# Contexts of a sequence taken in one visit instead of two, with eight buffers of turned probabilities

## The reference

```
x = emb[inp]                                   # token rows are gathered
q, k, v = x @ Wq.T + bq, x @ Wk.T + bk, x @ Wv.T + bv
scores = einsum('bhqd,bhkd->bhqk', q, k) / sqrt(16)      # 16 heads of 16
h = (softmax(scores) @ v) @ Wo.T + bo
n = layernorm(h);  Bu = (n @ B_w.T) @ C_w.T
h = h + sigmoid(n @ gate_w.T + gate_b) * exclusive_scan(decay, Bu)
h = h + layernorm(h) @ sign(weight).T
```

## Time and profile before

| | before |
|---|---|
| median of three runs | 829.03 us |
| the profiled execution's own time | 831.48 us |
| its span, first to last instruction | 829.4 us |
| mean granted TensorE clock | 0.979 |
| TensorE busy | 732.2 us (88%) |
| VectorE busy | 585.2 us (71%) |
| ScalarE busy | 580.9 us (70%) |
| GpSimd busy | 130.0 us (16%) |
| chain that ended last | PE 65%, issue 14%, DVE 9%, ACT 4% |

### The profile page before, as it was taken

The page is one execution under the profiler, slowest core; times in us unless marked ns, Lnnn a source line. Parts: engine busy times, 40 slices in busy tenths (PEclk is TensorE's granted clock), DMA queues, the critical chain, the costliest instruction groups (busy, mean ns, idle before and its releaser), DMA issues.

```text
span 829.4 us, 21108 instructions
## 1 busy us (share of the span) xinstructions
PE 732.2 (88%) x7047; PEld 650.2 (78%) x7047; DVE 585.2 (71%) x1307; ACT 580.9 (70%) x1643; POOL 130.0 (16%) x205
## 2 busy tenths in 40 slices
PE   1489999999999999999999999999999999999864
PEld 0378888888888888888888888888888888888754
DVE  4345677776677777777777787777777777787763
ACT  2178887777778877777787777777777777777710
POOL 7110111111110111111101111111011111100000
PEclk9889999999999999999999999999999999999977
DMA  4222223222322332223222312332232123322000
GB/s 128 89 90 77 90 91 103 69 73 91 102 91 91 97 101 61 72 95 101 93 93 92 101 56 71 101 101 89 88 101 95 56 76 101 101 89 81 23 13 26
DMA packets 56015, 69.67 MB, mean 84 GB/s; under 512 B 6768, under 2 KB 41648, under 8 KB 55984
## 3 DMA queue, kind: packets, MB, share of 16 engines
q1 hardware_dynamic: 52048, 60.48, 21.3%
q0 software_dynamic: 3072, 8.39, 4.9%
q10 hardware_dynamic: 864, 0.40, 0.2%
HBM read 10.52 MB, written 8.39 MB: 23 GB/s over the span
## 4 chain that ended last, share of the span: by engine, by line
PE 65%; issue 14%; DVE 9%; ACT 4%; SPq 3%; DMA 3%; POOL 1%; ACTq 0%; DVEq 0%; POOLq 0%
PE ps_g L623 32%; PE ps_t L695 10%; PE ps_g L672 8%; PE ps_c L623 7%; PE ps_s L623 6%; SPq L234 3%; DVE xn L519 2%; DVE h L583 2%; DVE gated L578 2%; ACT xTh L364 2%; PE ps_g L721 2%; DMA q_stack<-q_low 2%; SPq L239 1%; DMA gb_row<-in_gate_b 1%; DVE raw L452 1%
## 5 line engine op out<-in xcount | busy, mean ns | idle before, releaser
L338 ACT ACTIVATE probs<-ps_s,neg_max 128x128 f32<-128x128 f32 x1024 | 299.6, 400 | 73.6 <-DVE neg_max L486 73.6
L486 DVE TENSOR_REDUCE neg_max<-ps_s 128x4 f32<-128x512 f32 x256 | 176.4, 689 | 130.8 <-PE ps_s L623 128.7
L347 ACT COPY probsT<-ps_t 128x512 f32<-128x512 f32 x256 | 155.6, 608 | 43.1 <-PE ps_t L695 42.3
L695 PE MATMUL ps_t<-ident,probs 128*128 128x128 f32 x1024 | 154.4, 273 | 4.3 <-ACT probsT L347 4.2
L623 PE MATMUL ps_s<-k_stack,q_stack 128*128 128x256 f32 x512 | 124.3, 325 | 7.5 <-DMA q_stack<-q_low 7.5
L695 PEld LDWEIGHTS ps_t<-ident,probs 128*128 128x128 f32 x1024 | 119.6, 142 | 6.3 <-ACT probs L338 3.4
L286 POOL TENSOR_TENSOR rs<-ve,neg_half 128x2 f32<-128x2 f32 x32 | 22.2, 693 | 445.3 <-DVE ve L513 445.3
L623 PEld LDWEIGHTS ps_s<-k_stack,q_stack 128*128 128x128 f32 x512 | 78.1, 193 | 9.1 <-DMA q_stack<-q_low 9.0
L623 PE MATMUL ps_c<-probsT,v_aug 128*32 128x128 f32 x2048 | 83.1, 280 | 0.3 <-ACT probsT L347 0.3
L364 ACT CAST xTh<-ps_g 128x512 fp32r<-128x512 f32 x32 | 18.8, 586 | 77.8 <-PE ps_g L672 77.7
L721 PE MATMUL ps_g<-ident,ctx_raw 128*128 128x128 f32 x256 | 40.5, 281 | 34.5 <-ACT ctx_raw L357 34.5
(11 more groups left out here) (120 smaller groups left out, 1847.1 us busy)
## 6 DMA issues: line engine op xcount, KB each, us to landing
k_stack<-k_high SPq DMA_DIRECT2D x128, 128.0 KB, 2.4
q_stack<-q_high SPq DMA_DIRECT2D x64, 256.0 KB, 2.5
k_stack<-k_low SPq DMA_DIRECT2D x64, 128.0 KB, 2.3
q_stack<-q_low SPq DMA_DIRECT2D x32, 256.0 KB, 2.5
out<-y SPq DMA_DIRECT2D x32, 256.0 KB, 2.1
x_emb<-in_emb,id_col POOLq DMA_INDIRECT x64, 3.6
raw<-in_wkT SPq DMA_DIRECT2D x1, 256.0 KB, 3.0
raw<-in_wqT SPq DMA_DIRECT2D x1, 256.0 KB, 3.8
```

The costliest lines, as they stand in the source:

```text
L338: last = nc.scalar.activation(probs[s % 2][:, j], ps_s[s % 2][:, j * SEQ:j * SEQ + SEQ], ACT.Exp, bias=neg_max[s % 2][:, j:j + 1])
L347: nc.scalar.copy(probsT[st % 4][:], ps_t[:]).then_inc(act_pT, 1)
L486: nc.vector.tensor_reduce(neg_max[s % 2][:], ps_s[s % 2][:].rearrange("p (h k) -> p h k", h=HPS), axis=AX.X, op=ALU.max, negate=True).then ...
L695: last = nc.tensor.transpose(ps_t[:, j * SEQ:j * SEQ + SEQ], probs[st % 2][:, j], ident[:])
```

## The change

The two contexts per visit in four visits become four contexts per visit in two visits, in steps 2 and 6. The contexts of the second sequence (steps 4 to 7) run in step 2 of the next turn, those of the first (steps 0 to 3) in step 6. `probsT` gets a buffer for each of the eight steps, and a copy into it waits for the context of the same step one turn before. Nothing else moves; ScalarE's copies of `ps_c` keep their places.

```diff
-        probsT = [sb(f"probsT{p}", [P, HPS, SEQ]) for p in range(4)]
+        probsT = [sb(f"probsT{p}", [P, HPS, SEQ]) for p in range(8)]
@@ move_probsT
                         await_event(act, pe_pT, STEPS, pair, st + 1)
-                        await_event(act, pe_pv, STEPS, *after_four(pair, st))
-                        nc.scalar.copy(probsT[st % 4][:], ps_t[:]).then_inc(act_pT, 1)
-
-                def after_four(pair, st):
-                    p4, s4 = before(pair, st, 4)
-                    return p4, s4 + 1
+                        await_event(act, pe_pv, STEPS, pair - 1, st + 1)
+                        nc.scalar.copy(probsT[st][:], ps_t[:]).then_inc(act_pT, 1)
@@ context
-                    for back in (4, 3):
+                    for back in (6, 5, 4, 3):
@@
-                                      v_aug[vp][:, b, g * HPS + j], probsT[st % 4][:, j])
+                                      v_aug[vp][:, b, g * HPS + j], probsT[st][:, j])
@@ attention
-                    if s % 2 == 0:
+                    if s in (2, 6):
                         context(s)
```

## The result

| | before | after |
|---|---|---|
| median of 4 runs each | 828.74 us | 842.97 us |
| ratio to before, 95% interval | | 1.0169 (1.0152 to 1.0186) |
| the profiled execution's own time / its span | 831.48 / 829.4 us | 841.08 / 839.0 us |

The change makes the kernel 14 us slower. I had forecast 828.0 with a range of 810 to 836. The two profiled executions lie 9.6 us apart, less than the medians: the one of before took longer than any of its four timed runs, the one of after was the fastest of its four.

The account below looks back on a forecast made before the run. TensorE, 88% busy, was taken to set the pace for most of a turn, with another chain doing so at one place. Terms of -0.22, -0.25 and +0.44 gave -0.03 us per loop turn, about -1 us overall: 828.0 us, range 810 to 836.

Parts of the forecast that it names:

- A visit costs 0.76 us, a further step 0.22: TensorE's context visits: steps 0 and 4 each lose 0.76 us, steps 2 and 6 each gain 0.44.
- Step 0 to the second context rows hangs on the gather, which `y` holds: First part of a loop turn: `y` on VectorE lets the gather move only 0.22 us earlier; gain 0.22 us.
- Of step 4's 0.76 us 0.25 remain, cut off by `ctx_tok`: Second context rows to `ctx_tok` transposes: 0.25 us gained, the rest becoming a wait of about 0.45 us on VectorE's `ctx_tok`.
- From there on TensorE sets the pace and step 6's 0.44 us are paid in full: `ctx_tok` transposes to the next step 0: no TensorE wait, so step 6's longer visit adds 0.44 us.
- The other full turns balance alike, with about -0.2 us in their first part: Full turns outside the loop (3 to 5, 30, 31): balance like loop turns, first part about -0.2 us.
- The eight buffers cost nothing: Eight buffers of turned probabilities: no added instruction, and the copy's wait for the earlier context is over long since.
- The sum for a loop turn: Three parts of one loop turn added: -0.22 - 0.25 + 0.44 = -0.03 us, 24 times -0.7.
- the whole saving: Rival: nothing holds TensorE back, so 0.64 us arrives in each of 30 full turns, 19 us, 810; chance 0.10.
- the lifted signal: Rival: TensorE's late signal in step 2 goes, 0.69 us in each of 24 turns, 17 us, 811; chance 0.16.
- The slow one: Rival: the `x_emb` transposes' signal comes one slot later, 0.69 us per loop turn, 17 us, 845; chance 0.14.

## Why the prediction was wrong, point by point

- *A visit costs 0.76 us, a further step 0.22.* Right: 32 records take 1.08 us, 0.64 + 2 x 0.22, and from the gate to the next step 0, where step 6 lies, it is 453.97 - 446.80 = 7.17 us before and 435.31 - 427.71 = 7.60 after.
- *Step 0 to the second context rows hangs on the gather, which `y` holds.* Right: the gather moved to the predicted place. Of the gain of 0.22 us about 0.12 arrived in the loop, since the cast fell further behind the gather (2.94 us on average, 2.77 before). This term was off by 0.1 us. Why the cast fell back is open.
- *Of step 4's 0.76 us 0.25 remain, cut off by `ctx_tok`.* **This step failed.** The wait on `ctx_tok` is real, and the transposes did come 0.31 us earlier. But the working stopped there. The next group of TensorE, the gate, is held by `k_low`, and the timeline of before shows it: `k_low` ends 0.05 us ahead of the gate. A saving has to be followed to the next place where TensorE meets another engine, and then past it. The term is 0, not -0.25.
- *From there on TensorE sets the pace and step 6's 0.44 us are paid in full.* Right, shown twice (+14.4 with the double visit in step 6, -7.0 with the visit shortened).
- *The other full turns balance alike, with about -0.2 us in their first part.* **This failed too.** From the cast in turn 1 to that in turn 6 it is 110.9 us before and 114.6 after; it is 112.5 with the double visit in step 6 alone and 113.8 with the one in step 2 alone. Before, the signal was on time in turns 3, 4 and 5. After, it is late in all of them, and in turn 2 by more than before.
- *The eight buffers cost nothing.* Right (0.9995).

Turn 2 of both kernels, before and then after, shows that last failure at its largest. The cast starts 1.31 us after the gather in one and 2.82 in the other; in turn 4 it is 1.84 and 2.82:

```profile
83.98 1.04 POOL L277 DMA_INDIRECT x_emb<-in_emb,id_col  x1 [0.19 <-issue]
...
85.29 0.59 ACT L364 CAST xTh<-ps_g 128x512 fp32r<-128x512 f32 x1 [1.11 <-PE ps_g L672]
```

```profile
81.97 1.04 POOL L277 DMA_INDIRECT x_emb<-in_emb,id_col  x1 [0.19 <-issue]
...
84.79 0.59 ACT L360 CAST xTh<-ps_g 128x512 fp32r<-128x512 f32 x1 [2.61 <-remote]
```

The sum for a loop turn was -0.22 - 0.25 + 0.44 = -0.03. The traces have -0.12 + 0 + 0.43 = +0.31, which is 7.4 us in 24 turns, half of the 14. The stretch from turn 1 to turn 6 adds 3.7 us, and what follows the cast of turn 29 adds 0.9. That makes 12; the other 2 lie within what executions of one kernel differ by, and no trace assigns them. So it is partly chance that the double visit in step 6 alone costs the same 14 us: adding the one in step 2 gains 0.16 us per loop turn (24.24 to 24.08) and loses it again ahead of the loop.

Of the rivals, the whole saving and the lifted signal did not come. The slow one forecast nearly the measured time, 845, for a reason that the loop refutes: the double visit in step 2 alone, where it would act, makes the loop turn no longer. Its mechanism did act in the written-out turns 2 to 5, where I had priced nothing for it.

## What to carry to other kernels

Before work is taken off the busiest engine at one place and put down at another, ask of each place separately whether its time is exposed; the count saved says nothing. A quick test is to shorten the same work in either place by a known amount. Where the pace passes between engines, find the stretches whose length does not change (here 7.91 us from the cast to the gate), for taking work out of such a stretch gained nothing here, and work outside it was paid in full. Turns outside the loop are worth a look of their own: the few between turn 1 and turn 6 made a quarter of this loss. And look at waits in the starts of instructions: modelled ends hide gaps of some tenths.

## What the runs showed of the hardware

- In the loop TensorE's signals arrive late while GpSimd's indirect gather is under way: the cast that waits for them starts 0.8 us after the modelled end, 0.1 with plain transfers from SyncE in place of the gathers, and that replacement brought 22 us (0.9741). The delay is tied to the gather and moves to whichever signal falls into it: the `x_emb` transposes, or the visit's own once those are early.
- The delay takes steps rather than any value: with early transposes the copy that waits for the visit starts 2.13 to 2.20 us after the gather in 16 loop turns and 2.86 to 2.90 in eight of the same trace; with a double visit in step 2 it is about 2.95 in all (403.00 - 400.06 = 2.94). Why is open; the number of signals is not it, since one in place of four left the change at 1.0176.
- Shortening the moved width of the 128*32 matmuls from 128 to 32 columns halved a visit (0.64 to 0.33 us), it did not quarter it.
